# New first steps, a new last output and new orders of all engines in a one-core attention and FFN block

## What is computed

```python
x = x + layernorm(attn(layernorm(x)))      # 16 heads of 16, rotary positions, causal softmax
x = x + layernorm(ffn(layernorm(x)))       # H = gelu((x @ U1) @ V1 + b1); y = (H @ U2) @ V2 + b2
# attn: qkv = x @ qkv_w.T + qkv_b; q, k = rope(q), rope(k)
#       softmax(where(causal, -inf, q @ k.T / 4)) @ v, then @ proj_w.T + proj_b
# ffn: D 256, rank 64, inner 1024
```

## Time and profile before

| | |
|---|---|
| runs shown | 1219.38 us (median of 3) |
| profiled execution | 1223.06 us, its span 1221.3 us |
| TensorE busy | 1163.8 us (95%) |
| DVE, ACT | 945.8 us, 942.9 us (77% each) |
| POOL | 658.7 us (54%) |
| DMA | 142.22 MB, 51.8% of 16 engines' span on the main queue |

### The profile page before, as it was taken

The page is one execution under the profiler, slowest core; times in us unless marked ns, Lnnn a source line. Parts: engine busy times, 40 slices in busy tenths (PEclk is TensorE's granted clock), DMA queues, the critical chain, the costliest instruction groups (busy, mean ns, idle before and its releaser), DMA issues.

```text
span 1221.3 us, 25835 instructions
## 1 busy us (share of the span) xinstructions
PE 1163.8 (95%) x9845; PEld 620.9 (51%) x9845; DVE 945.8 (77%) x1452; ACT 942.9 (77%) x1898; POOL 658.7 (54%) x724
## 2 busy tenths in 40 slices
PE   5789999999999999999999999999999999999994
PEld 3545446554564456445554564455545444455452
DVE  7788887788878886779588958896788887567665
ACT  4357887688868887888779877987688699668784
POOL 2275514963497339832984289338923433336656
PEclk9889999999999999999999999999999999999997
DMA  5757644647545734674477537745565654302412
GB/s 166 209 78 151 142 67 79 144 112 122 113 128 133 137 81 126 133 104 117 103 165 108 130 90 164 116 124 112 106 124 93 123 110 125 107 1 96 147 70 104
DMA packets 99259, 142.22 MB, mean 116 GB/s; under 512 B 24896, under 2 KB 60992, under 8 KB 99136
## 3 DMA queue, kind: packets, MB, share of 16 engines
q1 hardware_dynamic: 99136, 140.58, 51.8%
HBM read 79.70 MB, written 51.38 MB: 107 GB/s over the span
## 4 chain that ended last, share of the span: by engine, by line
PE 62%; POOL 10%; DVE 8%; DMA 6%; SPq 6%; ACT 5%; issue 3%; POOLq 0%; ACTq 0%; DVEq 0%
PE PV L853 16%; PE RING L835 13%; PE RING L800 11%; PE RING L755 4%; PE RING L905 3%; DMA QK<-split_parts 3%; PE RING L864 3%; PE RING L898 3%; PE RING L767 3%; ACT PB L1170 3%; DVE MB L986 3%; SPq L628 2%; PE RING L806 2%; SPq L612 2%; POOL TB L538 2%
## 5 line engine op out<-in xcount | busy, mean ns | idle before, releaser
L1170 ACT ACTIVATE PB<-RING 128x512 f32<-128x512 f32 (+2 forms) x1280 | 623.9, 566 | 143.0 <-PE RING L835 129.9
L986 DVE TENSOR_REDUCE MB<-RING 128x2 f32<-128x1024 f32 (+2 forms) x448 | 497.5, 1142 | 102.8 <-PE RING L806 55.5
L835 PE MATMUL RING<-QK 64*128 64x512 f32 (+3 forms) x1536 | 318.2, 395 | 6.2 <-DMA QK<-NSROW 2.7
L1261 POOL TENSOR_SCALAR_AFFINE_SELECT PB<-PB 128x512 f32<-128x512 f32 x256 | 160.7, 638 | 282.7 <-ACT PB L1170 282.4
L800 PE MATMUL RING<-QK 62*128 62x512 f32 (+3 forms) x1536 | 294.4, 391 | 9.8 <-DMA QK<-split_parts 5.4
L835 PEld LDWEIGHTS RING<-QK 64*128 64x128 f32 x1536 | 168.9, 188 | 157.6 <-ACT PB L1170 95.1
L986 DVE TENSOR_REDUCE M<-RING 128x2 f32<-128x768 f32 (+1 forms) x186 | 191.1, 1042 | 60.8 <-PE RING L806 59.8
L853 PE MATMUL PV<-PB,VL 128*32 128x512 f32 (+3 forms) x2048 | 224.3, 523 | 0.6
L800 PEld LDWEIGHTS RING<-QK 62*128 62x128 f32 x1536 | 153.1, 188 | 130.3 <-DVE MB L986 36.4
L806 PE MATMUL RING<-MASKK,MASKQ 64*128 64x128 bf16 (+1 forms) x768 | 108.6, 248 | 0.0
L1195 ACT ACTIVATE F_H<-RING,F_B 128x512 f32<-128x512 f32 x128 | 80.5, 692 | 21.4 <-PE RING L898 21.2
(11 more groups left out here) (127 smaller groups left out, 1517.9 us busy)
## 6 DMA issues: line engine op xcount, KB each, us to landing
QK<-split_parts SPq DMA_DIRECT2D x372, 128.0 KB, 5.7
split_parts<-PARTS SPq DMA_DIRECT2D x60, 256.0 KB, 3.1
split_parts<-EO SPq DMA_DIRECT2D x60, 256.0 KB, 3.6
ATT<-OT SPq DMA_DIRECT2D x128, 64.0 KB
INV<-inverse_sums SPq DMA_DIRECT2D x32, 256.0 KB
block_mid<-Y SPq DMA_DIRECT2D x16, 512.0 KB, 3.1
F_X<-block_mid SPq DMA_DIRECT2D x16, 512.0 KB, 5.7
out<-F_Y SPq DMA_DIRECT2D x32, 256.0 KB, 2.2
```

What stands on the lines that cost most here:

```text
L835: ins = e.matmul(m[:, i, :], QK[g % 3][r, 1, k, 128 * j:128 * j + 128], QK[g % 3][r, 0, k, 512 * c + off:512 * c + 512], start=True, stop= ...
L986: e.tensor_reduce(acc, ring(("max", g, s, u), pairs, n), AX.X, ALU.max).then_inc(v_max, 1)
L1170: e.activation(buf[:, h, pairs[0]:pairs[-1] + 1, :], strip(("score", g, s, u), pairs, n), ACT.Exp).then_inc(a_exp, 1)
L1261: e.affine_select(buf[:, :, 0:128], buf[:, :, 0:128], pattern=[[0, 4], [1, 128]], base=0, channel_multiplier=-1, compare_op=ALU.is_ge, fil ...
```

## The change

- The rounding of the weights (`w_high`, before it stood ahead of ACT's string) becomes a step of that string, behind the first four `ln_rows`.
- In half (0, 0) DVE, not POOL, makes VE and NM, behind `ln_dev`; POOL keeps the power and the product.
- The turned rows of half (0, 1) go to a place of their own in QK[2] (`turned`), so `xt_out` of it waits for no product of half (0, 0); the `ones` of QK[2] now wait for the products of batch 0's both halves.
- `load_group` of group 0 (two steps of 12 DMAs, a half each, for Q and K together) becomes four steps `load_first` of 6 DMAs, K and Q apart, each of which waits for its own parts alone.
- The last `f_y` (7, 1) writes two banks of `up` in place of YP, and so needs not wait for `f_y_out` of (7, 0), but for all gelus; in the last batch DVE makes yv and yn behind `f_spread`, and POOL keeps the power and the product.
- ORDERS of all five engines and PLACES are new. One `warm` of two is gone. SP begins with the load of X2; in the last batch DVE takes out both tiles of `f_y` before the first `f_spread` is complete, and both `f_norm` come before both `f_res`.

```diff
-        "load_group": [(0, 0), (0, 1)] + [(g, None) for g in groups if g],
+        "load_first": [(c, p) for c in range(2) for p in (1, 0)],
+        "load_group": [(g,) for g in groups if g],
...
+        XTS = [[XTH, XTL], [QK[2][:, 0, :, 0:512], QK[2][:, 1, :, 0:512]]]
...
+        def turned(b, c):
+            return XTS[(b, c) == (0, 1)]
...
+        def y_banks(i, u):
+            return GP[0] if (i, u) == (NB - 1, 1) else YP
...
+                elif what == "load_first":
+                    c, p = at
+                    span = slice(512 * c, 512 * c + 512)
+                    w.wait_ge(*parts_sent(0, c, p))
+                    w.wait_ge(g_ones, 2)
+                    for t, term in enumerate(TERMS_K if p else TERMS_Q):
+                        src = split[0, term, p, 0:4, :, span].rearrange("(k h) f t -> h f k t", h=2)
+                        for h in range(2):
+                            r0 = 64 * h + 16 * t
+                            e.dma_start(QK[0][r0:r0 + 16, p, :, span].bitcast(fp32), src[h]).then_inc(s_ld0 if c == 0 else s_ld[0], 16)
...
                     w.wait_ge(o_mi["proj"], 4 * NB)
-                    w.wait_ge(f_y, 2 * (NTH[step] - 1))
+                    w.wait_ge(f_y, 2 * (NTH[step] - 1 - (y_banks(i, u) is not YP)))
+                    if y_banks(i, u) is not YP:
+                        w.wait_ge(f_g, 16 * NB)
...
                     ins.then_inc(v_ag, 1)
+                    if (b, c) == (0, 0):
+                        w.wait_ge(v_ag, 1)
+                        e.tensor_scalar(VE[:, :], MV[:, :, 1], EPS, None, ALU.add).then_inc(g_ve, 1)
+                        e.tensor_scalar(NM[:, :], MV[:, :, 0], -1.0, None, ALU.mult).then_inc(g_ve, 1)
...
                     ins.then_inc(f_yag, 1)
+                    if i == NB - 1:
+                        w.wait_ge(f_yag, NTH["f_spread", i, js])
...
+                        e.tensor_scalar(yv, mv[:, :, :, 1], EPS, None, ALU.add).then_inc(v_last, 1)
+                        e.tensor_scalar(yn, mv[:, :, :, 0], -1.0, None, ALU.mult).then_inc(v_last, 1)
...
-            w.wait_ge(a_cst, 1)
-            w.wait_ge(s_wq, 16)
-            e.activation(WQH[:, :, :], WQS, ACT.Copy).then_inc(a_wq, 1)
             for step in ORDER["ACT"]:
                 what, *at = step
-                if what == "ln_rows":
+                if what == "w_high":
+                    w.wait_ge(s_wq, 16)
+                    e.activation(WQH[:, :, :], WQS, ACT.Copy).then_inc(a_wq, 1)
+                elif what == "ln_rows":
...
-                    half = 2 * b + c
-                    w.wait_ge(p_mi["qk"], 8 * half)
-                    w.wait_ge(p_mi["values"], 4 * half)
-                    e.activation(XTH[:, k, :], BANKS[BANK["xt", b, c, k][0]], ACT.Copy).then_inc(a_xt, 1)
+                    used = {(0, 1): 0, (1, 0): 1}.get((b, c), 2 * b + c)
+                    w.wait_ge(p_mi["qk"], 8 * used)
+                    w.wait_ge(p_mi["values"], 4 * used)
+                    e.activation(turned(b, c)[0][:, k, :], BANKS[BANK["xt", b, c, k][0]], ACT.Copy).then_inc(a_xt, 1)
...
+                    if at[0] == 2:
+                        w.wait_ge(p_mi["qk"], 16)
+                        w.wait_ge(p_mi["values"], 8)
                     ones(*at)
```

More of the change, by code:

```diff
@@ L148 @@
                f="f_pow", F="f_ypow", A="f_res"),
-    "SP": dict(x="load_x", s="send", g="load_group", h="shift", a="att_load", m="att_sums", o="att_out",
+    "SP": dict(x="load_x", s="send", f="load_first", g="load_group", h="shift", a="att_load", m="att_sums", o="att_out",
                b="att_spread", t="store", L="f_load", I="f_fill", R="f_rest", S="f_store", N="f_next",
@@ L612, in sync @@
                             e.dma_start(dst.rearrange("h f t -> h f t"), src).then_inc(parts_sent(b, c, p)[0], 16)
+                elif what == "load_first":
[8 more added lines that the diff above has]
+                            e.dma_start(QK[0][r0:r0 + 16, p, :, span].bitcast(fp32), src[h]).then_inc(s_ld0 if c == 0 else s_ld[0], 16)
                 elif what == "load_group":
-                    g, c = at
+                    g, = at
                     b, h0 = g // 4, 4 * (g % 4)
-                    span = slice(0, NT) if c is None else slice(512 * c, 512 * c + 512)
                     for p in range(2):
-                        for i in range(2) if c is None else (c,):
-                            w.wait_ge(*parts_sent(b, i, p))
+                        for c in range(2):
+                            w.wait_ge(*parts_sent(b, c, p))
                     w.wait_ge(g_ones, 2 * min(g, 2) + 2)
@@ L625, in sync @@
                             for h in range(2):
[L626 removed]
+                                src = split[b % 2, terms[t], which, h0:h0 + 4, :, :].rearrange("(k h) f t -> h f k t", h=2)
                                 r0 = 64 * h + 16 * t
[L628 to L629 removed]
+                                e.dma_start(QK[g % 3][r0:r0 + 16, which, :, :].bitcast(fp32), src[h]).then_inc(s_ld[g % 3], 16)
                 elif what == "shift":
@@ L753, in tensor @@
                     bank = BANKS[BANK[step][0]]
-                    for n, (wq, xt) in enumerate(((WQH, XTH), (WQH, XTL), (WQL, XTH))):
+                    high, low = turned(b, c)
+                    for n, (wq, xt) in enumerate(((WQH, high), (WQH, low), (WQL, high))):
                         ins = e.matmul(bank, wq[:, k, 128 * m:128 * m + 128], xt[:, k, :],
@@ L764, in tensor @@
                     m, q = BANKS[BANK[step][0]][:, 256 * (j % 2):256 * (j % 2) + 256], 128 * (j % 4)
+                    high, low = turned(b, j // 4)
                     for k in range(2):
-                        for n, (xt, wq) in enumerate(((XTH, WQH), (XTL, WQH), (XTH, WQL))):
+                        for n, (xt, wq) in enumerate(((high, WQH), (low, WQH), (high, WQL))):
                             ins = e.matmul(m, xt[:, k, q:q + 128], wq[:, k, 512:768],
@@ L918, in tensor @@
                             r = slice(64 * a, 64 * a + 64)
-                            ins = e.matmul(YP[a][:, 256 * j:256 * j + 256], FQ[i % 2][r, q:q + 128], V2[r, :], start=True, stop=True)
+                            ins = e.matmul(y_banks(i, u)[a][:, 256 * j:256 * j + 256], FQ[i % 2][r, q:q + 128], V2[r, :], start=True, stop=True)
                     ins.then_inc(f_v2, 1)
@@ L939, in vector @@
                     w.wait_ge(a_xt, NTH["xt_out", b, c, k])
-                    e.tensor_tensor(XTL[:, k, :], BANKS[BANK["xt", b, c, k][0]], XTH[:, k, :].bitcast(fp32),
+                    high, low = turned(b, c)
+                    e.tensor_tensor(low[:, k, :], BANKS[BANK["xt", b, c, k][0]], high[:, k, :].bitcast(fp32),
                                     ALU.subtract).then_inc(o_mi["xt"], 1)
@@ L1296, in gpsimd @@
                     yv, yr, yn, half = (t[:, :].rearrange("p (a j) -> p a j", a=2)[:, :, rows] for t in (YV, YR, YN, HALF))
-                    e.tensor_scalar(yv, mv[:, :, :, 1], EPS, None, ALU.add).then_inc(f_yve, 1)
-                    e.tensor_scalar(yn, mv[:, :, :, 0], -1.0, None, ALU.mult).then_inc(f_yve, 1)
-                    w.wait_ge(f_yve, 2 * NTH["f_spread", i, js])
+                    if i == NB - 1:
+                        w.wait_ge(v_last, 2 + 2 * HALVES.index(js))
+                    else:
+                        e.tensor_scalar(yv, mv[:, :, :, 1], EPS, None, ALU.add).then_inc(f_yve, 1)
+                        e.tensor_scalar(yn, mv[:, :, :, 0], -1.0, None, ALU.mult).then_inc(f_yve, 1)
+                        w.wait_ge(f_yve, 2 * NTH["f_spread", i, js])
                     e.tensor_tensor(yr, yv, half, ALU.pow).then_inc(f_ypow, 1)
```

198 lines of the change are left out of this document (100 added, 98 removed).

## The result

The changed kernel takes 1207.57 us (median of 4 runs, 1204.79 to 1209.73), the kernel before 1221.26 beside it (4 runs, 1219.23 to 1224.67): a ratio of 0.9877, interval 0.985 to 0.9904. The sign was right, the size a third. The medians of the experiments leave out one run, of e3, which took 2234.98 us.

What follows compares the result with a forecast made beforehand. TensorE was taken to bound the middle, chains through other engines the ends. Head -3.0, output -1.4, orders 0 made -4.4 us, from 1219.38 to 1215.0; own range 1213 to 1217.5, 8 in 10 within 1209.5 to 1221.

Steps and rivals of the forecast that it cites:

- The head: Start to first score: gain 3.0 us, bounds 0.7 and 5.5; first score at 61.4, not 64.47.
- (a): First half of first batch: weights rounded behind normalisation, DVE makes VE and NM; first Q/K product 0.1 us later.
- (c): Split loads and shift rows: loads gain 2.5 us, X2's early load 0.5; first maximum 44.5, not 47.5.
- (b): Second half's own turned copy: products 1.1 us earlier, rotation up to 2.6 us earlier; memsets' price 0.
- So I carry it whole: Behind the first score: the head's 3.0 us lasts in full, as DVE's idle time moves with the first maximum.
- (e): All orders and bank places drawn anew: 0 us, bounds -6 and +8.
- The tail: Last output, last f_y on banks left by up: gain 1.4 us, 0.3 taken off for a held power.
- What would show it: Right: first maximum 44 to 45, first score 61 to 62, last sum 12.2; wrong: over five middle QK load waits.
- The middle gets better: Rival, middle: the new order removes a third of the idle 18.1 us, total 1210; chance 0.18.
- Late loads: Rival, middle: group loads 1.2 us late at seven batch changes cost 8.4 us, total 1223.4; chance 0.10.
- The head's gain absorbed: Rival, head: DVE or the memsets absorb its gain, only the tail's 1.4 us is left, total 1218.0; chance 0.22.
- The clock: Rival: shorter idle time before the first score spares a low-clock slice, total 1212.0, or the other way; chance 0.12.

Runs made afterwards that it cites:

- e3: Kernel before with the new last output only (banks of the last f_y, small operations on DVE, its orders): 1221.15 us, ratio 0.9996.
- e7: Changed kernel with the load of X2 issued behind the first two sends again, as before: 1216.0 us, ratio to before 0.9956.
- e12: Kernel before with one edit, X2's load as SP's first step after the constants: 1225.18 us, ratio 1.0024.
- e8: Changed kernel with the turned rows of half (0, 1) in XTH and XTL again: 1210.41 us, ratio to before 0.9921.
- e5: The changed kernel itself run again, beside the others on one chip: 1208.6 us, ratio to before 0.9898.
- e6: Changed kernel with each of the four split loads waiting for the parts of both Q and K: 1215.32 us, ratio to before 0.9957.
- e10: Kernel before with new orders from the first up of feed-forward batch 3 to the last output: 1221.05 us, ratio 1.0003.
- e1: Kernel before with the new first steps and new orders up to about 140 us, the rest and the output old: 1215.66 us, ratio 0.9954.
- e4: Kernel before with the new first steps and new orders up to 55 to 75 us only, the rest old: 1216.98 us, ratio 0.9977.
- e15: Kernel before with new orders from about 57 us to 140 us, first steps old: 1219.75 us, ratio 0.999.
- e17: Kernel before with 18 zero-tile multiplications in TensorE's wait for the first maximum and 8 before the first score: 1223.81 us, ratio 1.0013.
- e13: Changed kernel with 14 more matmuls of zeros ahead of the first maximum: 1204.4 us, ratio to before 0.9873.
- e18: Changed kernel with its wait for the first maximum filled, the same kernel as e13 run once more: 1207.18 us, ratio to before 0.9881.

## Why the prediction was wrong, point by point

**The head.** Right in kind: K's loads go before Q's parts have landed, and no bound of (a) to (c) was broken. The first product came at 14.80 (14.65 forecast), the first maximum at 43.38 (44.5), the shift rows at 53.70 (55.0), the first score at 60.71 (61.4). The first maximum and the first score lie just under the 44 to 45 and 61 to 62 of the signs. The term that was mis-sized is the X2 load in (c): "I take 0.5", measured 3.25 on the changed kernel (e7) and 1.8 on the kernel before (e12). I had priced the emptier queues near nothing, although the transfers ran at 266 GB/s under the whole wait. Against it stand sends and loads that came about 1 us later than in my sum. The memsets beside the rotation cost nothing. One step of (c) had the wait wrong: "the eight shift rows no longer wait for SP, but for DVE's chain". It was DVE before (57.97) and SP after (53.65 against DVE's 53.36). The two legs are so close that the time came out near all the same, which is luck. That edit (b) alone moves nothing at the first score (e8) agrees with my reading that TensorE was not what ACT waited for; the up to 2.6 us that I had given to the second half don't come from the copy.

**"So I carry it whole", and (e), "0, bounds -6 and +8".** This is the step that failed. Every order counted for nothing, and that held nearly for the middle alone. The new orders bring 2.5 us behind the first score, 2.0 in the feed-forward part and 0.8 in the middle. With head 3.8 and output 1.9 that makes 11.0, and with at most 2.2 for the clock 11.0 to 13.2. Measured were 13.7 between medians and 15.0 by ratio, and in e5 13.0 and 12.5. These are distances between profiles; e6 and e7, which cost 6.7 and 7.4 us for one edit of the head, show that the parts do not simply add up. My argument counted steps and average distances, and took the waits of TensorE over 1136 us in one. An average over seven changes of batch says nothing of the ramp. The wait for F_XH, 2.3 us in two pieces, was the next row of the view of the earlier trace rows; it is a wait that an order can move (0.8 after, 0.9 in e10), and I had left it out as not being a load. And I held TensorE's busy time for fixed by the work. It isn't: the clock and the order change it at the same count.

**The tail.** Right in mechanism and within 0.5 us in size: 1.4 forecast, 1.9 measured (1.0 to 1.5 against the four old tails at a later fall of the clock). The 0.3 for a held power was not needed, since the power took its 1.04 us; the new chain is 11.7 us.

**What would show it.** Three signs came true: K's loads, DVE's third tile, TensorE idle 16.9 us. Three numbers fell outside: the first maximum, the first score, and the last sum 11.7 us behind the first tile, not 12.2. One named as wrong came with the gain: seven waits on loads of Q and K, not at most five, 5.4 us. A faster part waits more for loads that are no longer hidden; here such waits say what is last now, not that the time is worse.

**The rivals.** *The middle gets better* (0.18, 1210) was nearest, but the gain is at its two ends and not in it. *Late loads* has its place (1.8 us in one wait) but not its price. *The head's gain absorbed* is refuted by e1, and e4, with the old orders behind the new head, agrees (2.8 us by its ratio). *The clock* has a part that isn't shown in size: I priced one slice at 3 us, and the runs leave at most about 2.2. If it hangs on something, then on the order behind the first score and not on the head: e15 keeps the clock with the old head, e4 misses 5.1 us with the new, in one profile each.

The range failed because its low end, 1209.5, did not even hold (e)'s own bound: 1215.0 less 6 is 1209.0, and X2's full room, 3.4 more, makes 1205.6. Both bounds were written down and neither was kept.

## What to carry to other kernels

Where a tuned order is redrawn as a whole, read the bounding engine by stretch, ramp and each change of phase by itself, its waits and its busy time: an order can win there even if the steady middle has nothing. Compare two orders only between points at which both have done the same work, by their counts of records, and look at the joint for pauses that neither order has. A large load amid small ones on the path is priced at its bytes by the rate of those microseconds, until shown otherwise, and edits on two legs that join, here the split loads and X2, are summed only after asking which leg is last with the one alone. A mechanism is read where it acts: the shift rows came near their forecast time although the prediction had the wrong engine last.

## What the runs showed of the hardware

TensorE's granted clock fell to its lower level, 1.2 GHz, also amid work without long pauses. This row is of the kernel before; in the 10.2 us ahead of it (523.0 to 533.2) the engine was busy 9.03 us at full clock:

```profile
533.20:536.60 3.40, 3.40 (x21) 1.23 (x22) 1.93 (x4) 1.55 (x4) 0.64 (x1) 0.50 0.05 10
```

Between 187 us and the tail such stretches lie in 13 of the 20 profiles, at 533 and 871 us in this one, 264 in e3, 703 in e1, 897 in e5, none in the changed kernel's. Each of 3.4 us costs about 1.7: the busy time of the middle is 843.02 us with two of them and 839.27 with none.

Filling a wait with work did not keep the clock up. In e17 it fell at 43.5 us, in a wait of 2.25 us ahead of the filling, and stayed low under the filling, with TensorE busy from 44.7 us on:

```profile
44.00:51.00 7.00, 6.83 (x18) 2.47 (x19) 3.11 (x10) 1.24 (x3) 3.50 (x5) 0.55 0.93 298
51.00:58.00 7.00, 6.02 (x43) 3.68 (x41) 5.93 (x9) 0.69 (x1) 1.81 (x1) 1.00 0.46 130
```

It was full again from 50.3 us. In the changed kernel's head the filling came earlier, at 39.57 us in e13, and there it made the low stretch later and shorter: 46.2 to 53.0 us in e13 and 46.9 to 53.7 in e18, 6.8 us each, where ten kernels with the new first steps, edited or not, and no filling have 10.2 to 13.7 us from 40.8 to 43.9 on. The first score came no earlier by it (60.19 and 60.51, against 59.69 to 61.41 in six kernels with the new first steps unedited).

A small POOL operation, the negation that makes NM, took 1.29 us beside a DVE subtraction with two inputs in SBUF, where its like takes 0.23. The pair, of the kernel after:

```profile
31.95 1.22 DVE L558 TENSOR_TENSOR EO<-EO,PARTS 128x1024 f32<-128x1024 f32 x1
...
31.97 1.29 POOL L1288 TENSOR_SCALAR NM<-MV 128x4 f32<-128x4 f32 x1
...
34.80 3.68 POOL L1255 MEMSET QK<- 128x2048 f32 x2
```

The memsets, beside DVE operations of the same kind, took 3.68, as the 3.67 of the earlier trace rows. The Trainium skill's page "SBUF — State Buffer", section "Who interferes with whom", says that such a DVE instruction contends with a GpSimd instruction that reads SBUF and not with one that only writes; both rows agree, and the memset's is the first here to show it.
